# Time mix of a perceiver layer on one core: reordered value channels, paired 32-row products, a ring of three banks

## The reference

```
xx = shifted(x) - x
t5 = tanh((x + xx * maa_x) @ maa_w1)                 # 5 groups of 32
m  = t5[f] @ maa_w2[f]                               # f = 0..4: w, k, v, r, g
xw, xk, xv, xr, xg = x + xx * (maa_f + m[f])
r, k, v = xr @ Wr, xk @ Wk, xv @ Wv;  g = silu(xg @ Wg)
decay = exp(-exp(tdecay + tanh(xw @ td_w1) @ td_w2))
for t: kv = k_t[:, None] * v_t[None, :]              # per head, 8 x 8
       y_t = r_t @ (S + u * kv);  S = decay_t[:, None] * S + kv
out = (groupnorm_per_head(y) * ln_w + ln_b) * g @ Wo
```

## Time and profile before

| | |
|---|---|
| runs | 605.06, 614.62 and 604.7 us; median 605.06 |
| profiled execution | 605.98 us, of which the span from the first to the last instruction is 604.3 |
| busy in the span | TensorE 519.8 us (86%), VectorE 430.7 (71%), ScalarE 347.0 (57%), GpSimd 333.1 (55%) |
| mean granted TensorE clock | 0.927 |
| cross attention, time mix and routing, experts | about 0 to 271, 271 to 500, 500 to 604 us |

### The profile page before, as it was taken

One profiled execution on the slowest core, in us unless ns is written; L12 is line 12 of the kernel. 1 busy time (PEld: TensorE's weight loads), 2 busy tenths in 40 slices (PEclk: granted clock), 3 DMA queues, 4 the chain that ended last, 5 costly groups with the idle time before them and its releaser, 6 DMA issues. The chain is left out here.

```text
span 604.3 us, 14849 instructions
## 1 busy us (share of the span) xinstructions
PE 519.8 (86%) x4354; PEld 352.7 (58%) x4354; DVE 430.7 (71%) x910; ACT 347.0 (57%) x1035; POOL 333.1 (55%) x690
## 2 busy tenths in 40 slices
PE   3889999999999999978688978698769768999970
PEld 1567777777777777764123323332336548999960
DVE  7467888788878887758779489686993645666643
ACT  3678888888888888812540442614524434666530
POOL 4136666666666666625655557279474651444440
PEclk9989999999999999978869999989895787999995
DMA  9215563222222222109999000000000112222217
GB/s 215 55 54 174 177 166 88 78 78 69 71 77 78 69 71 68 36 1 174 164 187 142 0 2 1 0 14 13 9 19 18 36 37 54 66 66 65 65 35 208
DMA packets 80265, 45.34 MB, mean 75 GB/s; under 512 B 4762, under 2 KB 79092, under 8 KB 80228
## 3 DMA queue, kind: packets, MB, share of 16 engines
q1 hardware_dynamic: 77956, 40.20, 29.7%
q0 software_dynamic: 2272, 4.69, 2.3%
HBM read 29.09 MB, written 15.78 MB: 74 GB/s over the span
## 5 line engine op out<-in xcount | busy, mean ns | idle before, releaser
L578 ACT ACTIVATE probs<-psum,neg_max 128x289 f32<-128x289 f32 x256 | 125.8, 498 | 34.1 <-DVE neg_max L751 34.1
L751 DVE TENSOR_REDUCE neg_max<-psum 128x1 f32<-128x289 f32 (+1 forms) x192 | 95.4, 552 | 45.5 <-PE psum L684 45.5
L634 PE MATMUL psum<-ident,probs 128*128 128x128 f32 x512 | 83.5, 286 | 1.6 <-ACT probs L578 1.3
L634 PEld LDWEIGHTS psum<-ident,probs 128*128 128x128 f32 x512 | 59.9, 153 | 26.5 <-issue 24.4
L1669 POOL DMA_INDIRECT y_rows<-x_sq,dest_row x39 | 37.4, 958 | 53.9 <-DVE dest_row L1775 49.4
L1076 POOL TENSOR_TENSOR w_up<-recep,w_gate 128x496 f32<-128x496 f32 x32 | 43.2, 1351 | 38.0 <-DVE w_gate L1462 37.6
L469 POOL TENSOR_TENSOR inv_spread<-quad_of,inv_sum 128x128 f32<-128x128 f32 x64 | 25.5, 398 | 56.7 <-DVE inv_sum L747 56.7
L578 ACT ACTIVATION_READ_ACCUMULATOR probs<-psum,neg_max 128x1 f32 x256 | 50.5, 197 | 0.0
L684 PE MATMUL psum<-kT,q_heads 32*128 32x289 f32 x512 | 49.4, 454 | 0.6 <-ACT probs L578 0.6
L1100 POOL DMA_INDIRECT x_rows<-rows_out,slot_no x32 | 35.0, 1093 | 18.7 <-issue 18.6
L757 DVE COPY pT<-psum 128x512 f32<-128x512 f32 x64 | 43.5, 680 | 0.7 <-PE psum L634 0.7
(11 more groups left out here) (265 smaller groups left out, 1253.2 us busy)
## 6 DMA issues: line engine op xcount, KB each, us to landing
x_rows<-blank SPq DMA_DIRECT2D x1, 9815.0 KB, 59.7
k_in<-in_ctx SPq DMA_DIRECT2D x64, 128.0 KB, 2.6
v_in<-in_ctx SPq DMA_DIRECT2D x64, 128.0 KB, 2.6
xs<-x_rows SPq DMA_DIRECT2D x39, 65.0 KB, 1.8
w_gate<-in_L_ffn_Wg SPq DMA_DIRECT2D x1, 1408.0 KB, 7.9
w_up<-in_L_ffn_Wu SPq DMA_DIRECT2D x1, 1408.0 KB, 6.9
x_res<-in_x SPq DMA_DIRECT2D x4, 256.0 KB, 3.8
v_own<-in_ctx SPq DMA_DIRECT2D x2, 512.0 KB, 7.7
```

The costliest lines, as they stand in the source:

```text
L578: last = nc.scalar.activation(probs_of(par, gr), bank[S_BANK[gr]][:, 0:KEYS], ACT.Exp, bias=neg_max[:, par, gr:gr + 1], accum_out=row_sum[ ...
L634: last = pe.transpose(bank[PT_BANK[h]][:, P * (2 * k + c):P * (2 * k + c) + P], probs_of(par, 2 * h + k)[:, P * c:P * c + P], ident[:])
L751: nc.vector.tensor_reduce(neg_max[:, par, start:end], psum[:, start:end, 0:KEYS], AX.X, ALU.max, negate=True).then_inc(s_max, 1)
```

## The change

The value channels are reordered: `placed(j)` puts value channel j of all 16 heads on 16 partitions next to each other, 32 * (j % 4) + 16 * (j // 4). W_v, W_g, W_o's rows, the parameters of the group norm and the matrices are laid out in this order. The key, the receptance and the state stay as they were. So spreading channel j takes only the 32 rows 32 * (j % 4) and on, and one matrix serves four channels. A new entry, `pair`, issues the products of channels 2p and 2p+1 together: high, high, low, low, in two groups of rows and two banks. The mix products are entries of their own (`mix_product`), mostly two together. The ring PROD has three banks (4, 5 and 0). Hidden goes to banks 3 and 2, which the mix products share. `v` and `decay1` of the next block are projected in steps 7 and 6; `shift` and `bonus` stand before the steps; `hidden` is at step 0, `norm` at 1, `output` at 4, and `turn` to `top` are in steps 0 to 2. The two small VectorE instructions of the second layer norm in the loops go to ScalarE.

```diff
+def placed(j):
+    return 32 * (j % TILES_K) + H * (j // TILES_K)
...
+                out_rows = t["L0_attn_W_o"].rearrange("(h a g) c -> g a h c", a=2, g=TILES_K)
+                for j in range(D):
+                    at = placed(j)
+                    sp.dma_start(w_time[at:at + H, W_O, :], out_rows[j % TILES_K, j // TILES_K]).then_inc(s_time_w_in, 16)
...
-            PROD, Y, POST = (4, 5), bank[6], bank[7]
+            HIDDEN, HIDDEN_LAST, MIX = bank[3], bank[2], (2, 3)
+            PROD, Y, POST = (4, 5, 0), bank[6], bank[7]
...
+            def turned(n):
+                return bank[1] if n < NB - 2 else bank[0]
...
             for n in range(NB):
                 r = n - 2
+                order.append(("project", n, "k"))
                 if n:
                     order.append(("y", n - 1, D - 2))
+                order.append(("project", n, "r"))
+                if n + 1 < NB:
+                    order.append(("shift", n + 1))
+                if n:
+                    order += [("y", n - 1, D - 1), ("centre", n - 1)]
+                order += [("project", n, "decay2"), ("bonus_in", n)]
+                if r == 1:
+                    order += [("scatter", 0, k) for k in range(4, TOP * TPB)]
+                order += [("project", n, "g"), ("bonus", n)]
                 if r >= 0:
                     order.append(("rows", r))
+                order.append(("pair", n, 0))
                 for j in range(D):
                     order.append(("state", n, j))
+                    if j == 0:
+                        if n + 1 < NB:
+                            order.append(("hidden", n + 1))
+                        if n:
+                            order.append(("variance", n - 1))
+                        order.append(("pair", n, 1))
+                        if r >= 0:
+                            order += [("turn", r), ("turned_T", r), ("turned_high", r)]
+                    elif j == 1:
+                        if r >= 0:
+                            order += [("logits", r), ("top", r, 0)]
+                    elif j == 2:
+                        order.append(("pair", n, 2))
+                        if n + 1 < NB:
+                            order += [("mix_product", n + 1, 0), ("mix_product", n + 1, 1)]
+                        if r >= 0:
+                            order.append(("top", r, 1))
+                    elif j == 4:
+                        order.append(("pair", n, 3))
+                        if n + 1 < NB:
+                            order += [("mix_product", n + 1, 2), ("mix_product", n + 1, 3)]
+                    elif j == 6 and n + 1 < NB:
+                        order.append(("mix_product", n + 1, 4))
+                    if r >= 0:
+                        order += {2: [("gap", r), ("places", r), ("turned_rows", r)], 3: [("slots", r)]}.get(j, [])
...
                     if j >= LAG:
                         order.append(("y", n, j - LAG))
                     if n:
+                        closing = {1: "norm", 3: "gated", 4: "output", 5: "ln_centre", 6: "ln_variance"}
                         if j in closing:
                             order.append((closing[j], n - 1))
...
+                    if r >= 0 and 4 <= j:
+                        order.append(("scatter", r, j - 4))
+                    if j == 3:
                         order.append(("add_bonus", n))
+                    if n + 1 < NB:
+                        if 2 <= j < 7:
+                            order.append(("mix", n + 1, j - 2))
+                        if j == 6:
+                            order.append(("project", n + 1, "decay1"))
+                        elif j == 7:
+                            order.append(("project", n + 1, "v"))
...
             def prod_bank(key_):
-                return bank[PROD[prod_no[key_] % 2]]
+                return bank[PROD[prod_no[key_] % len(PROD)]]
...
+                    elif s[0] == "ln_variance":
+                        act.wait_ge(s_ln_sqsum, 2 * NB + n + 1)
+                        nc.scalar.activation(ln_var[:, tiles_in(n)], ln_sqsum[:, tiles_in(n)], ACT.Copy,
+                                             scale=1.0 / C, bias=LN_EPS).then_inc(s_ln_var, 1)
...
+                    elif s[0] == "pair":
                         pe.wait_ge(s_spread_value, 1)
                         pe.wait_ge(s_value_low, n + 1)
+                        columns = (2 * s[2], 2 * s[2] + 1)
+                        for part in (value_high, value_low):
+                            for j in columns:
+                                key_ = ("state", n, j)
+                                rows = slice(32 * (j % TILES_K), 32 * (j % TILES_K) + 32)
+                                if part is value_high:
+                                    bank_free(key_)
+                                last = pe.matmul(prod_bank(key_), spread_value[rows, j // TILES_K, :], part[rows, :],
+                                                 start=part is value_high, stop=part is value_low)
+                                if part is value_low:
+                                    last.then_inc(s_prod, 1)
```

More of the change, by code:

```diff
@@ L922, in tiles_in, with early @@
                 return slice(TPB * n, TPB * n + TPB)
-            def mixing(n):
-                return [("hidden", n)] + [("mix", n, f) for f in range(5)]
+            def turned(n):
+                return bank[1] if n < NB - 2 else bank[0]
+            def early(n):
+                return [("hidden", n), ("mix", n, 0), ("mix", n, 1), ("mix", n, 2), ("mix", n, 3), ("mix", n, 4)]
             order = [("shift", 0), ("high", 0, 9), ("high", 9, len(splits)), ("low", 0, 4)]
-            for k, s in enumerate(mixing(0)):
+            for k, s in enumerate(early(0)):
+                if s[0] == "mix":
+                    order += {0: [("mix_product", 0, 0), ("mix_product", 0, 1)], 2: [("mix_product", 0, 2), ("mix_product", 0, 3)],
+                              4: [("mix_product", 0, 4)]}.get(s[2], [])
                 order += [s, ("low", 4 + 2 * k, 6 + 2 * k)]
+                if s == ("mix", 0, 2):
+                    order.append(("project", 0, "decay1"))
+                elif s == ("mix", 0, 3):
+                    order.append(("project", 0, "v"))
             order.append(("low", 16, len(splits)))
@@ L966, in perceiver_layer @@
                     if n:
-                        closing = {0: "variance", 2: "norm", 3: "gated"}
-                        closing.update({4: "output", 5: "ln_centre", 6: "ln_variance"} if n == NB - 1 else
-                                       {5: "output", 6: "ln_centre", 7: "ln_variance"})
+                        closing = {1: "norm", 3: "gated", 4: "output", 5: "ln_centre", 6: "ln_variance"}
                         if j in closing:
                             order.append((closing[j], n - 1))
-                    if r >= 0 and j == 0:
-                        order.append(("gap", r))
@@ L987, in perceiver_layer @@
+                    if n + 1 < NB:
[5 more added lines that the diff above has]
+                            order.append(("project", n + 1, "v"))
             last, r = NB - 1, NB - 2
-            order += [("scatter", r - 1, k) for k in (6, 7)]
-            order += [("y", last, D - 2), ("rows", r), ("turn", r), ("y", last, D - 1), ("turned_T", r), ("centre", last),
+            order += [("scatter", r - 1, k) for k in range(4, TOP * TPB)]
@@ L990, in perceiver_layer @@
+            order += [("rows", r), ("y", last, D - 2), ("turn", r), ("y", last, D - 1), ("turned_T", r), ("centre", last),
                       ("tile_list", last), ("variance", last), ("logits", r), ("top", r, 0), ("shared_down", 0), ("norm", last),
@@ L1260, in _ @@
                     par = n % 2
-                    if s == ("mix", 0, 0):
+                    if s == ("mix_product", 0, 0):
                         keep_busy(1)
@@ L1395, in _ @@
                 ln_vector(v, 1)
-                v.wait_ge(s_params, 1)
+                v.wait_ge(s_params, 2)
                 done = [0]
```

137 lines of the change are left out of this document (70 added, 67 removed).

## The result

The changed kernel took 646.55 us (median of 4 executions, 637.3 to 648.73), the kernel before 609.84 beside it on the same chip (604.7 to 614.84). The ratio is 1.0638, with an interval of 1.0428 to 1.0847: slower, and by more than the forecast's upper bound of 638. An execution at a mean granted clock of 0.892 took 637.3, two at 0.865 took 646.4 and 646.7, so the time of one and the same program goes with the clock. It also means that a total in this spread of 9 us proves little of a single edit; its waits in the profile do.

A forecast was written before the change was run, and what follows sets the result against it. VectorE's order was taken to bound the loops, TensorE closely behind. Loops +13.4, between -2.5, before block 0 +3.0, edits at nothing -0.2 and clock +4.5 sum to 18.2 over 605.06, so 623 us; range 604 to 638.

The forecast's parts named there:

- VectorE's own work, 92.3 us: Four step loops: VectorE's instructions summed as if nothing waited, 92.3 us in place of 103.8, a gain of 11.5.
- The waits, 24.9 us: Four step loops: idle VectorE time added by the new order at mix, output, norm and top, 24.9 us.
- Norm: Block 1, step 1: norm waits 3.4 us, as ScalarE does hidden before the variance's table loads and activations.
- top: Step 1: turned rows are copied behind ScalarE's table loads, so top waits 4.8 us in block 2, 2.1 in block 3.
- output: Step 4: output's products queue behind pair 3, mix products and y; 3.6 us wait in blocks 1 and 2, 2.7 in 3.
- mix: Steps 2 and 4: mix products queue behind a pair that waits for a scan, 1.5 us of idle VectorE.
- Between the loops, a gain of 2.5: Stretches between loops: 31.5 us in place of 34.0, with VectorE queued behind ScalarE's first column of diff.
- Before block 0, 3.0: Before the first loop: the chain over diff's column costs up to 3.5 us more; 3.0 taken, bounds 0 and 4.
- the clock, 4.5, bounds 0 and 9: TensorE's gaps before bonus, pair 2 and logits lower its clock, doubling some products of blocks 1 and 2: 4.5 us.
- the clock did not stay up: Rival 1, on TensorE: the waits come but the clock stays up, 618.8 us; chance 0.20.
- rival 2: Spread products: row tiles don't overlap, lengthening mix waits and outputs by 5 us more, 628 us; chance 0.10.
- The waits were not short: Rival 3, loops: short waits, not slower; no waits 594 us, chance 0.08; half the waits 606, chance 0.20.

The follow-up runs named there:

- the four of them: Changed kernel with mix products before pairs, diff's first column at shift, variance before hidden, output at 5, plus norm at 2 and later routing: 614.79 us, ratio 1.0122.
- the run with fillers: Changed kernel with extra unused TensorE products in its gaps, computation otherwise kept: 637.77 us, ratio 1.046.
- the edit of it alone: Changed kernel with ScalarE making the first column of the next block's diff at shift, ahead of centre and the decay's exponentials: 637.73 us, ratio 1.0463.
- The four single edits: Changed kernel, one edit each: mix products before pairs, 640.25 us; diff's first column at shift, 637.73; output a step later, 640.55; variance before hidden, 639.28.

## Why the prediction was right in direction and too small

*VectorE's order bounds the loops*: right. Edits that change nothing but the order in which instructions are queued took 6.0 to 8.8 us each, and the four of them, with later steps for `norm` and the routing, 31.8.

*VectorE's own work, 92.3 us*: 134.4 - 38.8 = 95.6 were measured, an error of 3.3. It is all in loops 2 and 3. One instruction in each, `is_second` for 32 columns, took 1.26 us in place of 0.19, until GpSimd's read beside it was through (418.66 to 419.90): 2.1 of the 3.3.

*The waits, 24.9 us*: places, releasers and, at full clock, sizes right, as the run with fillers shows in loops 0 and 1 (11.5 us of waits measured there without the 0.27 of the hop, 11.5 forecast). *Norm*, *top*, *output* and *mix* were each taken apart by one edit. In the changed kernel they were 38.8. Block 2's output shows how: of the 3.6 worked out, 1.5 was for pair and mix products, and they took 1.52 (428.67 to 430.19); 0.9 was for y, which took 1.87 until output's first product, and 1.2 from there to the addition, which took 1.85. At half rate 5.2 comes out, and 5.29 was measured.

*Between the loops, a gain of 2.5*: a loss of 3.3. The chain over diff's column was right (the edit of it alone took 5.0 out of these stretches), but its products (2.07 for bonus) ran at half rate; with fillers, blocks 2 and 3 had the forecast's 10.6 and 9.2.

*Before block 0, 3.0*: 6.0, outside the bounds. From 297 to 327 us the granted clock is 0.54, and up to the first key product it is 0.50, where the kernel before was at half level to 311 us (0.52) but at 0.97 from there to its first key product:

```profile
297.00:327.00 30.00, 25.47 (x33) 6.49 (x33) 21.81 (x27) 7.33 (x12) 12.64 (x10) 0.54 1.07 170
```

There the forecast doubled nothing, although the gaps that the new chain makes stand in it too.

*The step that failed: the clock, 4.5, bounds 0 and 9.* Its mechanism was right and its size was not. I priced it on a handful of products behind the long gaps of blocks 1 and 2, as if TensorE were back at full rate soon after. The trace shows 0.71 to 0.80 as the mean of every loop and every stretch between, so that all seven stretches lie above the forecast, by 1.0 to 6.3 us, and the front by 3.0. Fillers alone took back 2.1 in front, 2.1, 3.0 and 1.7 in loops 0 to 2 and 2.5 and 2.5 in two stretches between: 14 us in these places, already three times the term, and more than its upper bound. The kernel lies 26.7 us above the forecast's other terms (40.4 - 13.7): 14 by these places, 3.3 by VectorE's own work, and some 9 stay open. That loops 2 and 3 (8.6 us of waits above the forecast) owe all of theirs to the clock is likely and not shown: there the fillers didn't bring the waits down to the forecast.

The rivals: the clock did not stay up. Row tiles do overlap (327.26); the mix wait of 2.10 in block 0 is what rival 2 priced, but by luck, for with fillers it is 1.45. The waits were not short. Why the clock counts for more than before: VectorE's waits now end on products that are issued late, where TensorE was ahead and its rate hid behind VectorE's. This is argued; that the kernel before gained nothing by fillers fits it.

## What to carry to other kernels

When an order takes the engine that bounds a loop past instructions whose operands come late, follow each of them through every queue that it stands in; the waits can be worked out to a few tenths of a us from the old trace. Then price them a second time with TensorE at half rate, in all stretches in which it newly waits for VectorE, for a TensorE that no longer runs ahead shows its clock in every wait. And don't judge an edit by the wait that it aims at alone: some of that wait came back at the next instruction (3.72 became 1.76 and 0.20). The four single edits gave 28.4 us added up, and 31.8 together, with `norm` and the routing later as well, so here they all but added up.

## Of the hardware, not expected

- Around gaps of 1.73 and 0.77 us and with 32-row spread products the granted clock was 0.71 in the first 7.3 us of block 0's loop; around 1.87 and 1.28 us with 128-row ones it was 1.00. Why is open; it may also lie in what ran before.
- TensorE stayed at half rate (0.50) from 297 us to the first key product at 320.75, while it was busy for 21.0 of these 23.75 us.
- Extra products raised the clock of the kernel before from 0.927 to 0.934 and made it 0.7% slower: they are no gain where TensorE's work is hidden.
- A VectorE instruction with both operands in SBUF took 3.91 us beside three GpSimd instructions in a row of 3.64 together, and 0.69 without. The Trainium skill, SBUF — State Buffer, section 🔬 SBUF: two separate sides, has the two engines take their shared port by an exclusive lock for a whole instruction. The trace agrees that VectorE is held up, but here for the length of three of GpSimd's instructions, not of one; the 1.26 us of `is_second` ended with a single one.
